# Two attention layers over an image: the value products of layer 0 in batches of four groups instead of two

## The reference

```python
# layer 0, per image: IC = 64 inner channels, n, m = positions
theta = einsum('ic,cn->ni', theta_w, x) + theta_b
phi   = einsum('ic,cn->in', phi_w, x) + phi_b[:, None]
g     = einsum('ic,cn->ni', g_w, x) + g_b
y     = softmax(theta @ phi, axis=-1) @ g            # (n, 64)
x     = einsum('ci,in->cn', W_w, y.T) + W_b[:, None] + x
# layer 1, per image: 128 channels throughout
q, k, v = Wq x + bq, Wk x + bk, Wv x + bv
x       = x + (softmax(q.T @ k / sqrt(128), axis=-1) @ v.T).T
```

## Time and profile before

| | |
|---|---|
| median of 3 runs | 3430.94 us (3430.82 to 3434.11) |
| time of the profiled execution | 3435.51 us |
| its span in the trace | 3433.7 us |
| TensorE busy (x matmuls) | 3336.5 us, 97% (x13124) |
| GpSimd busy | 2965.9 us, 86% |
| VectorE busy | 2100.6 us, 61% |
| ScalarE busy | 1671.5 us, 49% |

### The profile page before, as it was taken

One profiled execution on the slowest core, in us unless ns is written; L12 is line 12 of the kernel. 1 busy time (PEld: TensorE's weight loads), 2 busy tenths in 40 slices (PEclk: granted clock), 3 DMA queues, 4 the chain that ended last, 5 costly groups with the idle time before them and its releaser, 6 DMA issues.

```text
span 3433.7 us, 46684 instructions
## 1 busy us (share of the span) xinstructions
PE 3336.5 (97%) x13124; PEld 2113.4 (62%) x13124; DVE 2100.6 (61%) x3029; ACT 1671.5 (49%) x2241; POOL 2965.9 (86%) x1366
## 2 busy tenths in 40 slices
PE   6999999999999989999999998999999999999998
PEld 4555566666655556666655555666665555566665
DVE  4555576776555557676755555677675555666674
ACT  4455445444455544444445554544454555444444
POOL 4999699898989969898989996989898999688897
PEclk9999999999999999999999999999999999999999
DMA  1000000000000000000000000000000000000000
GB/s 43 13 18 19 28 10 22 12 22 16 19 19 16 19 23 16 16 19 19 13 19 19 19 16 23 19 13 21 16 19 13 19 19 16 19 13 16 13 13 10
DMA packets 34038, 61.73 MB, mean 18 GB/s; under 512 B 5280, under 2 KB 5920, under 8 KB 33568
## 3 DMA queue, kind: packets, MB, share of 16 engines
q1 hardware_dynamic: 33824, 59.23, 5.6%
HBM read 42.44 MB, written 16.78 MB: 17 GB/s over the span
## 4 chain that ended last, share of the span: by engine, by line
PE 91%; DVE 3%; issue 2%; POOL 2%; ACT 1%; SPq 0%; DVEq 0%; DMA 0%; ACTq 0%; POOLq 0%
PE acc_out L471 16%; PE rough L398 15%; PE acc_out L455 13%; PE scores L420 7%; PE scores L423 7%; PE scores L425 7%; PE scores L429 7%; PE scores L426 7%; PE acc_out L443 2%; PE acc_out L441 2%; PE acc_out L442 2%; DVE piece_max L793 2%; PE rough L380 2%; PE acc_out L492 1%; PE acc_out L386 1%
## 5 line engine op out<-in xcount | busy, mean ns | idle before, releaser
L280 POOL TENSOR_TENSOR sums<-sums,probs 128x1024 f32<-128x1024 f32 x886 | 2116.0, 2388 | 145.1 <-ACT probs L718 104.7
L793 DVE TENSOR_REDUCE piece_max<-rough 128x1 f32<-128x512 f32 x2024 | 1309.5, 684 | 649.1 <-PE rough L398 646.2
L810 DVE TENSOR_TENSOR probs<-scores,shift_rows 128x1024 f32<-128x1024 f32 x512 | 626.7, 1224 | 567.3 <-PE scores L429 543.2
L718 ACT ACTIVATE probs<-scores 128x1024 f32<-128x1024 f32 x512 | 520.1, 1025 | 672.8 <-PE scores L423 665.1
L711 ACT ACTIVATE probs<-probs 128x1024 f32<-128x1024 f32 x512 | 539.4, 1053 | 499.6 <-DVE probs L810 499.4
L914 POOL TENSOR_TENSOR p_lo<-probs,p_hi 128x1024 fp32r<-128x1024 f32 x192 | 459.2, 2392 | 188.0 <-ACT probs L711 187.7
L471 PE MATMUL acc_out<-probs,v_vals 128*128 128x512 f32 x1280 | 605.4, 595 | 0.0
L425 PE MATMUL scores<-qry_a,k_hi 128*128 128x512 f32 x1024 | 507.8, 496 | 0.0
L455 PE MATMUL acc_out<-probs,g_vals 128*64 128x512 f32 x2048 | 495.0, 605 | 0.0
L420 PE MATMUL scores<-qry_a,phi_a 128*128 128x512 f32 x1024 | 432.3, 422 | 0.0
L710 ACT ACTIVATE p_hi<-probs 128x1024 fp32r<-128x1024 f32 x192 | 203.3, 1059 | 441.0 <-DVE probs L810 397.2
(11 more groups left out here) (97 smaller groups left out, 2961.0 us busy)
## 6 DMA issues: line engine op xcount, KB each, us to landing
x_q<-x SPq DMA_DIRECT2D x32, 256.0 KB, 2.7
x_res<-x SPq DMA_DIRECT2D x32, 256.0 KB, 3.0
mid<-mid_new SPq DMA_DIRECT2D x32, 256.0 KB, 2.2
x_q<-mid SPq DMA_DIRECT2D x32, 256.0 KB, 2.7
x_res<-mid SPq DMA_DIRECT2D x32, 256.0 KB, 3.2
out<-result SPq DMA_DIRECT2D x32, 256.0 KB, 2.3
x_kv<-x SPq DMA_DIRECT2D x24, 256.0 KB, 2.7
probs<-x SPq DMA_DIRECT2D x2, 1024.0 KB, 6.0
```

The source lines that it names most:

```text
L280: eng.tensor_tensor(sums[:, parity], sums[:, parity], probs[:, s % P_BUFS], ALU.add).then_inc(s_plus, 1)
L793: nc.vector.reduce_max(piece_max[:, t, c:c + 1], src, AX.X).then_inc(s_reduced, 1)
L810: nc.vector.tensor_tensor(probs[:, s % P_BUFS].rearrange("p (h c) -> p h c", c=QB), scores[:, s % 2].rearrange("p (h c) -> p h c", c=QB), ...
```

## The change

One constant goes from 2 to 4, and with it the three conditions quoted above.

```diff
--- before.py
+++ after.py
@@ -20,7 +20,7 @@
 SUB = QB // P
 P_BUFS = 8
 LAG = 3
-BATCH = 2
+BATCH = 4
 BATCH_AT = 1
```

## The result

The changed kernel takes 3484.74 us (median of 4 runs, 3484.04 to 3486.17), the one before 3432.53 us (median of 4, 3430.82 to 3436.33): a ratio of 1.015, 95% interval 1.0134 to 1.0166. It is slower by 52 us. The forecast was 3480, slower by 49.

The account below looks back on a forecast made before the run. TensorE was taken as the bound (97% busy), GpSimd a floor of 40.0 us per block. Waits 18.0 + 22.1 + 10.7 + 42.6 = 93.4 less 44.6 gave +48.8, so 3480 us; 8-in-10 range 3452 to 3505.

Parts of the forecast that it names:

- The passage: Going into the 64-column form and out around a batch: 0.36 us each, 124 fewer, 44.6 us gained.
- The estimate with 166 ns: Passage priced by the skill's fixed latency part: gain only 20.6 us, time near 3504; not adopted.
- The rival with 1.17 us: Idle weight loads add 0.81 us to each passage's 0.36: 3379 us; chance 0.06 together with waits being hidden.
- The entry: Block start after the shift row, no batch covering qry_b and qry_a: 1.52 us in 28 blocks, 42.6 us lost.
- the rival in which the entry was covered after all: ScalarE reaches its copies earlier at block entry, so 42.6 us falls away: 3437, about no change; chance 0.06.
- rdiag: Step 8, L498 waits for ScalarE's rdiag: 0.58 us in 27 blocks, 1.61 in 4 turn blocks, 22.1 us lost.
- The pairs of pieces: Steps 2 to 4 and 6 to 8, pairs with one score group between: 2 x 0.28 us per block, 18.0 lost.
- Step 11: Third piece waits as finish precedes its reductions on VectorE: 0.40 us in 24 blocks; 10.7 us lost with first blocks.
- Step 5's scores: Scores directly following step 4's, needing exponential 3: no wait, but no margin either.
- the third rival: A further wait joins, such as step 5's scores: 16 to 32 us more, 3496 to 3512; chance 0.13.
- Item 3: Step 11's third piece: 0.40 us in 24 blocks, 0.28 in 4 first blocks, turn blocks nothing; 10.7 us.

Follow-up runs that it names:

- the two runs that take it from either side: Changed kernel, last batch cut in two at steps 15 and 1: 3448.97 us; kernel before, groups 12 and 13 moved to step 1's batch: 3464.68 us.
- The repair: Changed kernel with reciprocal rows at step 9 and normalise at step 10, in layer 0 blocks after another layer 0 block: 3463.72 us.
- the run with the order alone: Kernel before, batches of two, with the pieces of steps 3, 7 and 11 ahead of the scores: 3451.23 us.
- the best arrangement of batches of four with the old third pieces: Changed kernel with reciprocal rows at step 9 and the last batch cut in two at steps 15 and 1: 3430.01 us, ratio 0.9991.

## Why the prediction was right

**The passage** (forecast 0.36, 44.6 in all). The batch of step 9 takes 3.80 us in the changed trace, and the run with one passage more per batch gives 0.35. The estimate with 166 ns from the Trainium skill ("TensorE: Matmul & The Clock Gate", Single matmul latency) would have made the gain 24 us smaller; the run does not bear that out as the price of a passage. The rival with 1.17 us is refuted. The 0.81 us of idle weight loads is not time lost: in the changed trace the loads idle for 0.81 up to 1120.82, and the value products run on through all of it, the merged row from 1117.23 ending at 1120.88.

**The entry** (forecast 1.52 a block, 42.6). 1.64 and 1.55 by the two runs that take it from either side, and 2.74 - 0.23 - 0.92 = 1.59 in the timeline. Right, a little small: the rival in which the entry was covered after all is out. The 0.17 between the end of ScalarE's work and the start of the matmul that waits, which had no row, can now be read: 0.16 behind qry_b (1090.91 to 1091.07), 0.24 behind qry_a (1092.39 to 1092.63) and 0.16 behind rdiag (1114.90 to 1115.06).

**rdiag** (forecast 0.58 and 1.61, 22.1). 0.62 in the ordinary block shown. The repair, which leaves the 3 first blocks behind a layer 1 alone, gave 21.0 where the forecast's terms make 24 x 0.58 + 4 x 1.61 = 20.4. In the first turn block L498 waits:

```profile
393.54 0.50 PE L498 MATMUL acc_out<-rdiag,ones_r 128*128 128x512 f32 x1 [1.32 <-ACT rdiag L646]
```

Its start, 393.65, is 1.59 after the place that was free: the matmul ahead ended at 393.54 - 1.32 = 392.22, so it started at 391.83, and 392.06 was free.

**The pairs of pieces** (forecast 18.0). 16 to 19 us in the run with the order alone, 0.55 in an ordinary block.

**Step 11** (forecast 0.40, 10.7 in all) has no run of its own. In the timeline the third piece starts at 1124.89 + 0.50 - 0.39 = 1125.00, and 1124.32 + 0.23 = 1124.55 was free: 0.45.

**Step 5's scores**, priced at nothing with no margin, wait a little in the second image. The piece ahead is followed by step 4's scores, and then:

```profile
1102.94 0.46 PE L420 MATMUL scores<-qry_a,phi_a 128*128 128x512 f32 x1
```

The 0.46 in place of 0.39 is a start 0.07 late. That is the third rival, in the smallest size it could have.

**What was missed.** Three things, besides the short stretches at the lower clock, which the forecast read as none.

First, ScalarE's answers are slower in most blocks than in the one that was read: the exponential starts 0.51 us after the last score matmul (1099.68 to 1100.19) where the forecast had 0.42. The wait for qry_a, the one for rdiag, the third piece of step 11 and step 5's scores are each 0.06 to 0.09 us longer by it. That is most of the difference between blocks of 45.90 and 45.55. The forecast of 45.65 lies between them and is 0.25 short in 22 blocks.

Second, the turn blocks do pay for the missing batch at step 11. Item 3 says "Turn blocks pay nothing"; it walked the third piece, which they do not have, and not the keys, for which they wait 4.2 us.

Third, a gain at the end of the turn blocks. Before, the denominators there waited for the additions:

```profile
PE acc_out L492 <- DVE total L267: 4.7, 4, 1.2
```

In the changed kernel this line is gone: TensorE arrives later, and the sum that it needs is ready. So 4.7 us of the new waits cost nothing. I had walked GpSimd through the ordinary block only.

Cut from shift row to shift row and summed over both profiled executions, the difference lies here (us):

| | forecast | measured |
|---|---|---|
| 24 ordinary blocks | 38.9 | 43.8 |
| 4 turn blocks, with the hand-over to layer 1 | 9.0 | 7.4 |
| 4 first blocks | 0.8 | -0.4 |

The measured ones make 50.8. The block at the lower clock, which only the execution before has, takes off 1.7 of them: 49.1 in the spans. Stretches at the lower clock of different length lie in the last two rows too. Each forecast term is found at its place and near its size, step 11's in the timeline alone. That the total of 48.8 comes so near is partly luck, since the slower answers and the wait for the keys, some 9 us together, met a gain at the turn of 4.7 and the differences of the clock.

## What to carry to other kernels

A block of matmuls on the engine that sets the pace is also the time in which the others answer. Before such a block is moved or merged, list for each place that it leaves what is awaited right behind it, and hold its length against that latency: here 0.36 us per passage was won, and three covers of 2.08 us were taken away, of which 0.4 to 1.6 us each came back as waits. Do this for each kind of block: the turn blocks lost a cover that the ordinary ones did not need. Where pieces alternate over two buffers, it is their distances that count: a single third piece between two score groups cost nothing, while the same piece ahead of a pair cost 0.83 us, and moving the third pieces gained 29 us, where the best arrangement of batches of four with the old third pieces gained 3.

## What the runs showed of the hardware that was not expected

ScalarE mostly starts 0.42 to 0.44 us after the start of the last score matmul in the blocks 0, 5, 6 and 7 of the first image, and 0.50 to 0.52 after it at most places in its blocks 1 to 4 and in all blocks of the later images. The kernel before shows the same (989.05 to 989.55 in its second image, 334.73 to 335.15 in block 6 of the first). In the program the blocks 1 to 4 of a layer stand in a loop, and all later images in another; the four quick blocks are those of layer 0 that are written out outside of any loop. That this makes the difference was not tried.

Going into the 64-column form and out again costs 0.35 us here, whether 4 or 8 pairs lie between. A change between float32 and fp32r in the 128 x 128 form shows no such cost.
